# A graph network's gather kernel: products of layer 0 in two PSUM banks, their rows' copy in one, and later turns

## The chip, the cores and the metric

The kernel runs on one core of a Trainium2 chip. The metric is the device time of one execution in microseconds (us), lower is better; three runs of the kernel before gave a median of 2989.48 us (2987.55 to 3002.36). A core has five engines with a queue each: TensorE (PE in the profile, its weight loads PEld), VectorE (DVE), ScalarE (ACT), GpSimd (POOL) and SyncE (SP). They are tied together by semaphores: a counter that one engine raises and another waits for.

## The reference

Two graph layers over 6250 nodes with 512 features and 100000 edges sorted by target. Layer 0 sums each node's neighbours, and sends the sums through two dense products (512 to 1024 to 512) with a batch norm behind each; layer 1 has one product (512 to 512), a ReLU and a batch norm. Each ends in a residual and a row-wise layer norm.

```python
# layer 0
agg = segment_sum(x[src], dst, N);  h = (1 + eps) * x + agg
h = relu(batch_norm(h @ W1 + b1, g1, be1))
h = relu(batch_norm(h @ W2 + b2, g2, be2))
x = layernorm(x + (x + h))
# layer 1
agg = segment_sum(x[src], dst, N);  h = where(indeg > 0, agg, x)
h = relu(h @ W.T + b);  x = layernorm(x + batch_norm(h, gamma, beta))
```

## The kernel before

The program has five stages: `gather_phase` of layer 0, `hidden_phase` (the product with W2), `rows_phase` of layer 0, then `gather_phase` and `rows_phase` of layer 1.

**Gather.** Nodes come in 50 tiles of 125, worked off as 25 pairs. The edges come in 782 chunks of 128. For each chunk POOL issues one indirect DMA (L571) that fetches 128 rows of 512 numbers into one slot of a ring (34 slots in layer 0, 20 in layer 1). SP counts what has landed (L537). PE adds a chunk's rows to the tile's sums by a matmul with a selection matrix of zeros and ones (a tile looks at a window of 18 chunks), which DVE makes by comparisons (`selection`, L640 to L654). POOL may reuse a slot when PE's counter `used` says that its chunk is done (L586).

**Split rows.** A matmul in full fp32 takes four times the passes of one in the rounded format fp32r. So in layer 0 eight chunks of a window (two in layer 1) are split: ACT copies the rows rounded (`high_rows`, L929), and in layer 0 writes the same rounded rows once more into PSUM (L931, banks 5 and 7 in turn, `high_ps`); DVE subtracts that copy from the exact rows (`low_rows`, L670); PE multiplies both parts (L806, L811). The other ten chunks of a tile go as they are (L821, two records each in the profile). `AHEAD` says by how many rows ACT's copies may be ahead of DVE's subtractions: two, one for each bank. A tile's 18 steps stand in the order whole, whole, split, whole, split and so on, and end with a whole one.

**Turn and product.** When a pair's sums are complete, DVE adds the nodes' own rows (`read_sums`, L685). During the next pair, before step `TURN_AT` of its first tile, PE transposes them (`turn`, L839); ACT rounds the result (`high_part`, L916), DVE makes the low part (`low_part`, L693). The product with the layer's weights (`product`, L854) is cut into parts of 24 matmuls, four in layer 0 and two in layer 1, and `PRODUCT_AT` says behind which step of which tile each part stands. ACT reads a part out of PSUM (`read_product`, L943 and L946) and tells PE by `product_out` (L949); in layer 0 all parts use bank 4, so a part waits until the one before is read, while in layer 1 there are two banks. DVE takes the batch norm's statistics (L701). What an engine does in a pair is written out by hand, in L722 to L759 for DVE and L973 to L1011 for ACT; each engine works strictly in that order.

**Hidden and rows.** `hidden_phase` begins with the batch norm's constants (L1040: a square root on ACT), then rectifies the last pair's features, which are still on chip (`first`, L1126 for ACT and L1170 for DVE), and multiplies with W2 (L1214). `rows_phase` normalises blocks of features on ACT (`features`, L1323), PE turns them into rows (L1399), and DVE, ACT and POOL add the residual and do the layer norm.

## Time and profile before

| | |
|---|---|
| median of three runs | 2989.48 us (2987.55 to 3002.36) |
| the profiled execution's own time | 3012.35 us |
| its span, first to last instruction | 3010.6 us |
| granted TensorE clock, mean | 0.894 of full speed |
| PE busy, PEld busy | 81%, 54% |
| DVE, ACT, POOL busy | 46%, 32%, 51% |
| HBM | 181 GB/s over the span |

The profile is one execution. Busy shares are means over five stages with different limits, so a stage is read by itself: a window of the trace gives the busy time of each engine in it, the granted clock and the share of time in which the 16 DMA engines moved data. "Waited for" rows say how long an engine stood idle before an instruction and whose semaphore ended it; "issue" is idle time that no semaphore explains, and "remote" a semaphore whose raiser the profile did not find close by. The end of a matmul's record is modelled, its start is measured.

### The profile page before, as it was taken

What the parts mean: (1) busy time and instruction counts of PE and PEld (TensorE: products, weight loads), DVE (VectorE), ACT (ScalarE), POOL (GpSimd) and SP (SyncE); (2) the same over time, 40 slices, a digit from 0 to 9 for tenths busy, and PEclk for the clock granted to TensorE, in tenths of its full rate; (3) what the DMA queues carried; (4) which work ended last, traced back from release to release, by engine and by line L of the source; (5) the groups of instructions that cost most, each with busy time, mean ns of one, the idle gap of its engine ahead of it and who ended that gap; (6) DMA issues with size and microseconds to landing.
All of it is one profiled execution on the core that took longest, in us unless ns stands there. A gap on an engine that the chain in (4) does not pass through costs nothing. (4 is left out here: it accounts for less than half of the span.)

```text
span 3010.6 us, 42654 instructions
## 1 busy us (share of the span) xinstructions
PE 2427.2 (81%) x9711; PEld 1615.2 (54%) x9712; DVE 1370.1 (46%) x2159; ACT 955.1 (32%) x1674; POOL 1548.7 (51%) x1729
## 2 busy tenths in 40 slices
PE   3888778788887887799997497888779788877875
PEld 2555555556565655578886354444444444444445
DVE  4444444444443444453336554444344444444448
ACT  2444444444443443455555311010111011011026
POOL 6555656656555565500001465666566666666633
PEclk9989989999988898899998598989889898988986
DMA  7666656666666666632225765666666666666668
GB/s 242 183 194 185 206 170 203 191 204 188 202 184 195 181 205 184 184 94 95 95 95 151 248 189 171 184 183 177 177 180 181 190 183 183 188 180 180 175 175 270
DMA packets 180572, 545.12 MB, mean 181 GB/s; under 512 B 48787, under 2 KB 51178, under 8 KB 175794
## 3 DMA queue, kind: packets, MB, share of 16 engines
q0 software_dynamic: 125120, 410.09, 47.1%
q1 hardware_dynamic: 33880, 78.23, 8.8%
q10 hardware_dynamic: 21544, 56.48, 5.7%
q8 instruction: 11, 0.18, 0.0%
q14 instruction: 17, 0.14, 0.0%
HBM read 493.06 MB, written 51.62 MB: 181 GB/s over the span
## 5 line engine op out<-in xcount | busy, mean ns | idle before, releaser
L821 PE MATMUL psum<-ring,select 128*125 x2600 | 1270.1, 616 | 36.6 <-issue 36.4
L571 POOL DMA_INDIRECT ring<-x_in,staged x782 | 742.5, 950 | 522.9 <-issue 206.2
L571 POOL DMA_INDIRECT ring<-x_d,staged x782 | 751.3, 961 | 459.5 <-issue 219.7
L821 PEld LDWEIGHTS psum<-ring,select 128*125 128x125 f32 x2600 | 492.7, 196 | 440.7 <-issue 397.1
L854 PE MATMUL psum<-sumsT_hi,w_hi 128*128 128x250 f32 x1248 | 429.2, 344 | 244.8 <-ACTq L949 146.8
L670 DVE TENSOR_TENSOR rows_lo<-ring,psum 128x512 fp32r<-128x512 f32 x404 | 274.6, 686 | 425.4 <-ACT psum L931 352.5
L854 PEld LDWEIGHTS psum<-sumsT_hi,w_hi 128*128 128x128 f32 x1248 | 273.3, 219 | 318.7 <-ACTq L949 179.2
L929 ACT ACTIVATE rows_hi<-ring 128x512 fp32r x506 | 315.1, 628 | 315.0 <-issue 220.7
L854 PE MATMUL psum<-sumsT_lo,w_hi 128*128 128x250 f32 x1248 | 384.3, 308 | 7.0 <-issue 7.0
L854 PE MATMUL psum<-sumsT_hi,w_lo 128*128 128x250 f32 x1248 | 383.1, 307 | 7.6 <-issue 7.4
L806 PE MATMUL psum<-rows_hi,select_r 128*125 128x512 f32 x500 | 359.3, 719 | 13.1 <-issue 9.9
L854 PEld LDWEIGHTS psum<-sumsT_lo,w_hi 128*128 128x128 f32 x1248 | 275.4, 221 | 29.4 <-issue 29.3
L854 PEld LDWEIGHTS psum<-sumsT_hi,w_lo 128*128 128x128 f32 x1248 | 274.5, 220 | 6.1 <-issue 6.0
L943 ACT ACTIVATE of_layer<-psum,vecs 128x250 f32<-128x250 f32 x208 | 86.2, 466 | 494.2 <-remote 404.3
L931 ACT ACTIVATE psum<-ring 128x512 fp32r x404 | 236.6, 586 | 0.0
L916 ACT ACTIVATE sumsT_hi<-psum 128x500 fp32r<-128x500 f32 x104 | 55.5, 586 | 529.9 <-DMA ring<-x_in,staged 285.8
L1369 POOL TENSOR_TENSOR both_r<-six_r 125x5 f32<-125x5 f32 x18 | 3.6, 200 | 401.6 <-DVE six_r L1432 401.6
L681 DVE TENSOR_SCALAR lone<-psum 125x1 f32 (+1 forms) x51 | 8.1, 158 | 440.1 <-DMA x_d<-rows_r 203.3
L811 PE MATMUL psum<-rows_lo,select_r 128*125 128x512 f32 x500 | 202.0, 404 | 1.6 <-issue 1.6
L663 DVE TENSOR_REDUCE edge_count<-select 128x125 bf16<-128x2000 f32 x50 | 198.2, 3964 | 0.0
L946 ACT ACTIVATE h3T<-psum,vecs 128x250 f32 (+1 forms) x104 | 43.3, 468 | 478.1 <-DMA ring<-x_in,staged 365.0
L1214 PE MATMUL psum<-act_hi,w_hi 128*128 128x500 f32 (+1 forms) x416 | 160.3, 385 | 4.1 <-DVE act_lo L1172 4.1
(184 smaller groups left out, 2470.9 us busy)
## 6 DMA issues: line engine op xcount, KB each, us to landing
hidden_d<-of_layer ACTq DMA_DIRECT2D x25, 1000.0 KB
act_f<-hidden_d SPq DMA_DIRECT2D x24, 1000.0 KB
ring<-x_in,staged POOLq DMA_INDIRECT x782
ring<-x_d,staged POOLq DMA_INDIRECT x782
own<-x_in ACTq DMA_DIRECT2D x50, 224.0 KB
own<-x_d ACTq DMA_DIRECT2D x50, 224.0 KB
rows_r<-x_in SPq DMA_DIRECT2D x6, 1120.0 KB
x_d<-rows_r SPq DMA_DIRECT2D x6, 1120.0 KB
```

Source lines behind the costliest of these rows:

```text
L571: nc.gpsimd.indirect_dma_start(slot(s), None, table, bass.IndirectOffsetOnAxis(ap=staged[:, s:s + 1], axis=0)).then_inc(gathered[s], 16)
L663: nc.vector.tensor_reduce(edge_count[h][:, 1, :], select[h][:].rearrange("p k n -> p n k"), AX.X, ALU.add).then_inc(counted[h], 1)
L670: nc.vector.tensor_tensor(rows_lo[:, k, :], of_chunk(dve, first, SPLIT_AT[k]), high, ALU.subtract).then_inc(split_lo, 1)
L806: high = nc.tensor.matmul(agg(h), select_r[h][:, k, :], rows_hi[:, k, :], start=False, stop=False, skip_group_check=True)
L811: nc.tensor.matmul(agg(h), select_r[h][:, k, :], rows_lo[:, k, :], start=False, stop=False, skip_group_check=True).then_inc(split_used, 1)
L821: whole = nc.tensor.matmul(agg(h), select[h][:, WHOLE_AT.index(p), :], of_chunk(pe, first, place), start=False, stop=n + 1 == WINDOW, skip ...
L854: last = nc.tensor.matmul(out, w[:, k, o * P:(o + 1) * P], s[:, k, :], start=n == 0, stop=n == len(parts) - 1)
L916: nc.scalar.activation(sumsT_hi[:, b * z.KD // 2:(b + 1) * z.KD // 2, :], turn_ps[:, b, 0:z.W * z.KD // 2].rearrange("p (k n) -> p k n", n ...
L929: high = nc.scalar.activation(rows_hi[:, k, :], of_chunk(act, first, SPLIT_AT[k]), ACT.Copy)
L931: high = nc.scalar.activation(high_ps[k % 2].bitcast(F32R), of_chunk(act, first, SPLIT_AT[k]), ACT.Copy)
L943: nc.scalar.activation(hidden[:, o, :], from_, ACT.Identity, bias=m.b1[:, o:o + 1]).then_inc(out_done, 1)
L1214: last = nc.tensor.matmul(out, w[:, f * KK + k, o * P:(o + 1) * P], s[:, 0:pairs, k, :] if pairs == 2 else s[:, 0, k, :], start=f == 0 and ...
```

## The change

In layer 0 the parts of the product alternate between banks 4 and 7 (`prod_ps`), so that part b waits for the reading of part b-2; for that the rounded rows' copy in PSUM keeps bank 5 alone (`high_ps`), and ACT may be ahead of DVE by one row (`AHEAD` = 1). The turn stands before step 7 instead of 5 in layer 0 and before step 8 instead of 5 in layer 1. The parts of the product stand two steps later in layer 0; in layer 1 the first part goes from step 12 to the end of the first tile (18), the second from step 2 to step 6 of the second tile. ACT's readings and copies and DVE's subtractions, sums and statistics are put in another order to suit. A square root in setup has ACT's table loaded there. The first blocks of the hidden phase are handed from ACT to DVE to PE one by one, and in the rows phases the first four blocks of features are made by ACT (two), POOL and DVE.

The diff, cut to its core; in the order of its pieces: setup's square root, the steps, the banks, DVE's order in a pair, PE's wait for a bank, ACT's order in a pair, the hidden phase's first blocks on ACT, and the first blocks of the rows phases on POOL and DVE.

```diff
+        act.wait_ge(self.tables, 2)
+        nc.scalar.activation(self.root[:], m.bn_eps[:], ACT.Sqrt, bias=m.ln_eps[:, 0:1])
...
-    TURN_AT = 5
-    PRODUCT_AT = ({14: 0}, {2: 1, 8: 2, 14: 3}) if layer == 0 else ({12: 0}, {2: 1})
+    TURN_AT = 7 if layer == 0 else 8
+    PRODUCT_AT = ({16: 0}, {4: 1, 10: 2, 16: 3}) if layer == 0 else ({18: 0}, {6: 1})
...
-        high_ps = [m.bank(5), m.bank(7)]
-        AHEAD = 2 if layer == 0 else 0
-        PRODUCT_BANKS = 1 if layer == 0 else 2
-        def prod_ps(b, last):
-            return m.bank(4 if b % 2 == 0 or layer == 0 and not last else 0 if layer == 0 else 5)
+        high_ps = m.bank(5)
+        AHEAD = 1 if layer == 0 else 0
+        PRODUCT_BANKS = 2
+        def prod_ps(b):
+            return m.bank(4 if b % 2 == 0 else 7 if layer == 0 else 5)
...
-                            low_rows(v, 1, second, 0, 3)
+                            low_rows(v, 1, second, 0, 6)
                             read_sums(v, tiles(i, 0), 0)
-                            low_rows(v, 1, second, 3, 5)
...
-                            statistics(v, pair, 0, 2)
-                            low_rows(v, 1, second, 5, 7)
-                            statistics(v, pair, 2, 4)
-                            low_rows(v, 1, second, 7, SPLIT)
+                            low_rows(v, 1, second, 6, SPLIT)
+                            statistics(v, pair, 0, 4)
...
-                    pe.wait_ge(product_out, HALVES * job + b + (1 if layer == 1 or b == 0 or not final else 0))
+                    pe.wait_ge(product_out, HALVES * job + b + 1)
...
-                            high_rows(begin1, v, 1, second, 0, 3)
+                            high_rows(begin1, v, 1, second, 0, 4)
+                            load_own(v, tiles(i, 1), 1)
                             read_product(v, pair, 0)
-                            high_rows(begin1, v, 1, second, 3, 5)
-                            load_own(v, tiles(i, 1), 1)
+                            high_rows(begin1, v, 1, second, 4, 6)
                             read_product(v, pair, 1)
-                            high_rows(begin1, v, 1, second, 5, 7)
+                            high_rows(begin1, v, 1, second, 6, SPLIT)
...
+                            high_rows(following_begin, v + 1, 0, following, 0, 2)
                             read_product(v, pair, 2)
-                            high_rows(begin1, v, 1, second, 7, SPLIT)
-                            high_rows(following_begin, v + 1, 0, following, 0, EARLY)
+                            high_rows(following_begin, v + 1, 0, following, 2, EARLY)
                             read_product(v, pair, 3)
...
+                    for k in range(KK + 1):
+                        if k < KK:
+                            nc.scalar.activation(m.hidden[:, f * KK + k, :], m.hidden[:, f * KK + k, :], ACT.Relu,
...
+                        if k:
...
+                            nc.scalar.activation(act_hi[f][:, 0, k - 1, :], m.hidden[:, f * KK + k - 1, :], ACT.Copy
+                                                 ).then_inc(hi_done[f] if k == KK else first_hi, 1)
...
+        def first_features(engine, wait, k, line, done):
+            out = normed[0][:, k, :]
+            made = engine.tensor_scalar(out, featT[:, k, 0:SW], scale[:, k:k + 1], bias[:, k:k + 1], ALU.mult, ALU.add)
+            if layer == 0:
+                made.then_inc(line, 1)
+                wait.wait_ge(line, 1)
+                made = engine.tensor_scalar(out, out, 0.0, None, ALU.max)
+            made.then_inc(done, 1)
```

What this moves in the queues shows at three places. On PE, in the first tile of a pair in layer 0, ahead of the turn (L790 and L839 follow these rows; `rows_hi` and `rows_lo` are the split rows, `select_0` a tile's selection):

```order
 L821 MATMUL psum<-ring,select_0 125x512
 L805 ISA
+L806 MATMUL psum<-rows_hi,select_r_0 125x512
+L811 MATMUL psum<-rows_lo,select_r_0 125x512
+L820 REGISTER_ALU
+L821 ISA
+L821 MATMUL psum<-ring,select_0 125x512
+L805 REGISTER_ALU
 L806 MATMUL psum<-rows_hi,select_r_0 125x512
 L811 MATMUL psum<-rows_lo,select_r_0 125x512
```

One split and one whole step more stand in front of the turn; the same step pairs have gone from behind it, from in front of the product's parts.

On ACT, in the second tile of a pair in layer 0: L929 and L931 are one split row's two copies, L943 the reading of one part of the product (`of_layer` is where it goes), L910 the load of the tile's own rows. Before:

```order
L929 ACTIVATE rows_hi<-ring 128x512
L931 ACTIVATE psum<-ring 128x512
...
L943 ACTIVATE of_layer<-psum,vecs 128x250 x2
...
L929 ACTIVATE rows_hi<-ring 128x512
L931 ACTIVATE psum<-ring 128x512
...
L929 ACTIVATE rows_hi<-ring 128x512
L931 ACTIVATE psum<-ring 128x512
...
L910 DMA own_0<-x_in 112x512
L910 ISA
L910 DMA own_0<-x_in 13x512
...
L943 ACTIVATE of_layer<-psum,vecs 128x250 x2
```

and after:

```order
L929 ACTIVATE rows_hi<-ring 128x512
L931 ACTIVATE psum<-ring 128x512
L910 ISA
L910 DMA own_0<-x_in 112x512
L910 ISA
L910 DMA own_0<-x_in 13x512
...
L943 ACTIVATE of_layer<-psum,vecs 128x250 x2
...
L929 ACTIVATE rows_hi<-ring 128x512
L931 ACTIVATE psum<-ring 128x512
...
L929 ACTIVATE rows_hi<-ring 128x512
L931 ACTIVATE psum<-ring 128x512
...
L943 ACTIVATE of_layer<-psum,vecs 128x250 x2
```

The first reading now stands behind the tile's fourth split row instead of its third, the load of own rows stands in front of it, and the second reading is behind the sixth row instead of the fifth.

On ACT at the start of the program and of the hidden phase (L1040 is the square root of the batch norm's variance):

```order
+L215 ACT_TABLE_LOAD
+L215 ACTIVATE setup_root<-bn_eps,ln_eps 128x1
...
-L1040 ACT_TABLE_LOAD
 L1040 ACTIVATE bn_tmp<-bn_tmp,bn_eps 128x8
```

There are two table loads before and one after, which has moved from in front of the first copy of setup to in front of the added root.

## Rows read from the trace of the kernel before

**Rows 1.** Windows of the trace: the two gather stages, from first turn to last.

```profile
core 0: us, PE busy (x) PEld busy (x) DVE busy (x) ACT busy (x) POOL busy (x), PEclk, DMA share, GB/s
53.20:1270.10 1216.90, 982.38 (x4273) 679.57 (x4274) 531.24 (x912) 520.14 (x1010) 708.68 (x748) 0.91 0.65 192
1762.60:2913.20 1150.60, 948.66 (x3207) 529.72 (x3206) 508.87 (x671) 121.70 (x240) 709.69 (x739) 0.90 0.63 180
```

**Rows 2.** Timeline of PE (start us, us, engine line op): turns of layer 0's last pairs.

```profile
1270.11 1.91 PE L839 MATMUL psum<-ident,sums 125*128 125x125 f32 x8
...
1306.54 1.05 PE L839 MATMUL psum<-ident,sums 125*128 125x125 f32 x8 [1.02 <-DVE sums L685]
```

**Rows 3.** Waits (us in total, times, longest) of PE: layer 0's gather, then layer 1's.

```profile
PE psum L854 <- ACTq L949: 146.8, 33, 10.5
PE psum L790 <- DVE sums L685: 60.5, 15, 5.4
...
PE psum L854 <- DVE sumsT_lo L693: 77.4, 12, 10.5
PE psum L790 <- DVE sums L685: 41.8, 5, 11.2
```

**Rows 4.** Waits of POOL in layer 0's gather.

```profile
POOL ring L571 <- PE psum L821: 162.7, 66, 10.8
POOL ring L571 <- remote: 149.0, 51, 4.3
```

**Rows 5.** Timeline around layer 0's third product of a pair, with gathers running.

```profile
637.21 0.68 PE L854 MATMUL psum<-sumsT_hi,w_hi 128*128 128x250 f32 x1
640.27 0.28 PE L854 MATMUL psum<-sumsT_hi,w_lo 128*128 128x250 f32 x1
...
644.72 0.95 POOL L571 DMA_INDIRECT ring<-x_in,staged  x1 [0.30 <-issue]
...
647.45 0.83 ACT L943 ACTIVATE of_layer<-psum,vecs 128x250 f32<-128x250 f32 x2 [9.00 <-remote]
...
648.38 0.38 PE L854 MATMUL psum<-sumsT_hi,w_hi 128*128 128x250 f32 x1 [3.87 <-ACTq L949]
648.41 0.95 POOL L571 DMA_INDIRECT ring<-x_in,staged  x1 [2.74 <-remote]
```

**Rows 6.** Timeline around a first product after the last gather.

```profile
1281.93 0.28 PE L854 MATMUL psum<-sumsT_hi,w_lo 128*128 128x250 f32 x1
...
1282.25 0.47 ACT L943 ACTIVATE of_layer<-psum,vecs 128x250 f32<-128x250 f32 x1 [0.89 <-PE psum L854]
```

**Rows 7.** Timeline of ACT and DVE: split rows, back to back and one by one.

```profile
615.05 0.63 ACT L929 ACTIVATE rows_hi<-ring 128x512 fp32r x1 [2.11 <-issue]
616.11 0.61 ACT L929 ACTIVATE rows_hi<-ring 128x512 fp32r x1
...
620.99 1.28 DVE L670 TENSOR_TENSOR rows_lo<-ring,psum 128x512 fp32r<-128x512 f32 x2
...
621.97 0.63 ACT L929 ACTIVATE rows_hi<-ring 128x512 fp32r x1 [2.35 <-DVE rows_lo L670]
622.51 0.59 ACT L931 ACTIVATE psum<-ring 128x512 fp32r x1
...
623.29 0.69 DVE L670 TENSOR_TENSOR rows_lo<-ring,psum 128x512 fp32r<-128x512 f32 x1 [1.02 <-ACT psum L931]
```

**Rows 8.** Timeline: ACT's first row after the loop's end; DVE's selection begins.

```profile
608.97 0.63 ACT L929 ACTIVATE rows_hi<-ring 128x512 fp32r x1 [1.86 <-issue]
...
618.01 0.23 DVE L640 TENSOR_SCALAR local<-dst_t,tile_bases 128x17 f32 x1
```

**Rows 9.** Timeline of the hidden phase's start.

```profile
1326.86 1.28 ACT L1040 ACT_TABLE_LOAD   x1 [4.06 <-PEq L88]
...
1329.34 2.06 ACT L1128 ACTIVATE of_layer<-of_layer,bias,scale 128x250 f32<-128x250 f32 x4 [0.87 <-DVE bias L1037]
...
1333.85 0.55 PE L1214 MATMUL psum<-act_hi,w_hi 128*128 128x250 f32 x1 [4.10 <-DVE act_lo L1172]
```

**Rows 10.** Timeline of PE: the rows phase's first transposes, layer 0.

```profile
1618.86 3.40 PE L1399 MATMUL psum<-ident,normed_r 128*125 128x128 f32 x14 [8.25 <-ACT normed_r L1325]
```

78 lines of the change are left out of this document (52 added, 26 removed).

## The prediction, made before the changed kernel was run

> **What bounds the kernel now.** I read the busy shares by slice first: two gather stages, one for each layer, take almost 80% of the span (1216.9 and 1150.6 us, PE's clock at 0.91 and 0.90 of full, DMA share 0.65 and 0.63) [rows 1]. Layer 0's runs from its first turn to its 25th, so 24 pairs at 1216.9 / 24 = 50.7 us; layer 1's 1150.6 / 24 = 47.9 us. PE is recorded busy for 982.4 of 1216.9 us. The waits say what it misses: 146.8 us for ACT's reading of the one product bank (ACTq L949) and 60.5 us for the sums that the turn needs; in layer 1, 77.4 us for the low part of the turned sums and 41.8 us for sums [rows 3].
>
> The timeline shows why. A product's 24 matmuls start at 637.21 and the last is recorded at 640.27; ACT, which has waited 9.00 us for its completion, starts to read at 647.45, and PE, which has gone on with gathered rows meanwhile, stands 3.87 us before the next product [rows 5]. POOL's last gather of that stretch starts at 644.72, the next at 648.41 after 2.74 us of waiting. So a product's completion is told some 7 us after its last record, shortly after the gather stream has run dry, and everything starts again then. After the last gather, a product whose last record is at 1281.93 is read at 1282.25, 0.3 us later [rows 6], and that whole pair takes 1306.54 - 1270.11 = 36.4 us [rows 2]. Hence 50.7 - 36.4 = 14.3 us of a pair are these late completions and what follows from them. POOL alone needs 1.25 us a gather (0.95 and 0.30 [rows 5]): 748 gathers in 24 pairs [rows 1] are 31.2 a pair, 39.0 us, and its waits are (162.7 + 149.0) / 24 = 13.0 us more [rows 4]; together about the pair's 50.7.
>
> I take the lateness as a fact of this kernel without knowing its cause. One rule speaks against reading it as idle time: the Trainium skill (Trace Analysis, "Tensor Engine Instruction") says that a matmul's end in the profile is computed, and that the semaphore moves only when PSUM has acknowledged all bytes. By that rule the array could still be working until 647.4, and a second bank would give nothing; that is rival C. Rows 2 and 6 speak against it, since the same work ends promptly and 14.3 us sooner without gathers.
>
> **Layer 0, what goes.** Two product banks let product b start once b-2 is read. Between products lie six steps of gathered rows plus a product, so the wait of 146.8 / 24 = 6.1 us a pair is mostly gone. The wait before the turn stays: the third product and the turn both move by two steps, their distance is the same, and the chain behind it (read, statistics, sums) is unchanged: 60.5 / 24 = 2.5 us a pair.
>
> **Layer 0, what comes.** The rounded rows' copy has one bank, so ACT's pair of copies for row k+1 waits until DVE has subtracted row k. Before, pairs follow each other every 616.11 - 615.05 = 1.06 us. One by one they cost [rows 7]: the pair from 621.97 to 622.51 + 0.59 = 623.10, 1.13 us; 0.19 us until DVE starts at 623.29; 0.69 us of DVE; and 0.3 us until ACT starts again (DVE's pair of rows from 620.99 has its first end near 621.68, ACT starts at 621.97). Sum 2.31 us, times 16 rows: 37.0 us. What lies between the rows, less what runs beside the other engine's part:
> - ACT's way round the loop, 1.86 us [rows 8] instead of 0.3, and DVE's sums: 1.8 us.
> - Turn, its high and low part: 1.0 to 2.7 us (the upper end is the 2.11 us that ACT stands before 615.05 [rows 7]).
> - DVE's two selections, each from 618.01 to 620.99, 3.0 us [rows 7, 8], of which the next copy hides 1.1 to 1.5; the second follows the sums and a register load: 1.5 + 3.1 us.
> - Four reads of products (0.83 us each [rows 5], each half hidden by a subtraction) and statistics: 1.3 us.
>
> Together 45.7 to 47.4, say 46.5 us a pair. This chain of ACT and DVE, hardly visible before (25 of 50 us), is now longer than POOL's 39.0 and PE's own work, below 36.4. It is the new bound.
>
> On top come completions that it can't cover. Reads stand 4 to 10 us behind their products in the new order, so the first three mostly fit (7 us late against 9 to 12 us of distance), while the fourth is read at once after the last row: some 2 to 3 us stay. I take 46.5 + 2.2 = 48.7 us. Bounds: 45.7 (all covered) and 46.5 + 7 = 53.5 (one full lateness of 7.2 us a pair on the chain). Against 50.7 that is -2.0 us (-5.0 to +2.8), over 24 pairs -48 us (-120 to +67). The last pair, without gathers, goes from 36.4 to about 46: +10 us. Layer 0: -38 us (-110 to +77).
>
> **Layer 1.** Turn from step 5 to 8, first product from 12 to the tile's end, second from 2 to 6; it had two banks already. PE comes 3 steps, some 2.6 us, later to the turn and 5.2 us later to the product, so the 77.4 us of waits for the low part (12 times, longest 10.5) and the 41.8 us for sums (5 times) [rows 3] shrink by at most 12 x 5.2 + 5 x 2.6 = 75 us. But work is only moved: POOL's 39 us and its pauses stay, and selection for the second tile, queued on DVE behind the low part, starts 2.6 us later with 3 us. It is covered by the product now in front of that tile. I take a third: -24 us (-60 to +10).
>
> **The short phases.** The square-root table is loaded in setup beside other waits; in front of the hidden phase it stood in the open for 1.28 us [rows 9], and the next instruction starts at its end: -1.3. The Trainium skill (ScalarE: Activation LUTs, "What ACT_TABLE_LOAD costs") puts a switch at 2.66 us with its drain; by that figure 1.4 us more would go, but the row shows no drain. Hidden phase: PE starts at 1333.85, 4.5 us after ACT's first block at 1329.34 [rows 9]; with blocks handed on singly it can start after two blocks, a copy and a subtraction, about 2 us, but then waits for each of the four: -1.5 (0 to -2.5). Eight small copies instead of two cost ACT up to 1 us, hidden by PE's first unit. Rows phases: PE waits 8.25 us for four ACT blocks [rows 10], of which two now go to DVE and POOL: -2 each (-1 to -2.5). Sum -7 us.
>
> **Sum.** -38 - 24 - 7 = -69 us on the profiled execution, whose own time is 3012.4 us (span 3010.6): 2943. The runs' median is 2989.5, a factor 0.992 below it, so 2921 us.
>
> **Rivals.**
> A, the forecast: the copy chain replaces the bank wait and is a little shorter. 0.45; 2921 us.
> B, slower: the single copy bank decides. If a product's completion on the ACT-DVE chain costs its whole lateness once a pair, the period is 53.5 us: +67 + 10 in layer 0. For it speaks that ACT reads in program order, so each late product stops all later copies and with them PE; against it, the new distances. It decides from a period of 50.7 us, 4.2 us of uncovered waiting on 46.5. With the other terms (-24 - 7) 3012 + 46 = 3058, median terms 3035 us. 0.25.
> C, nothing moves: the array is busy until the completion, as in the rule above, or the stream of gathers keeps its 39.0 + 13.0 us whatever PE does, because each product still ends in a pause. Layer 0 at 50.7, layer 1 unchanged, -7: 2983 us. Four products a pair and four pauses speak for it. 0.13.
> D, a large gain: PE runs on to the next product while the last is late, so that one pause flushes two, the chain covers all, period 46.0, and layer 1 gains 60: -113 + 10 - 60 - 7 = -170: 2821 us. Against it: each late product also freezes the counters that POOL and ACT wait for. 0.17.
>
> **Numbers.** 0.5% (15 us) is what a measurement of this kernel can tell from no change. Faster: 0.42 of A and all of D, 0.59; same: 0.03 of A and 0.11 of C, 0.14; slower: B and the rest of C, 0.27. Range: A's bounds alone are 2850 to 3000; with most of B and half of D, 2840 to 3038.
>
> **What would show it.** Right: the rows of PE's wait for ACTq L949 in layer 0 nearly gone; ACT's copy pairs at about 2.3 us, each begun by DVE's L673; PE waiting instead for rows_lo and for sums; turns 48 to 49 us apart; the pair after the last gather longer, near 46 us. Wrong: copies still close to 1.1 us apart (DVE never the releaser), or turns below 46 or above 51 us apart; in layer 1 the wait for the low part still at 77 us; a table load still in front of the hidden phase.

## The result and the profile after

The changed kernel took 2959.3 us (median of four, 2952.64 to 2964.52) against 2989.64 us for the kernel before on the same chip: a ratio of 0.9896, 95% interval 0.9869 to 0.9922. So it is faster, by 30 us, where 69 were forecast (2921 us). The experiments add a second finding that the forecast did not see coming: two chips were met in a second condition, in which the kernel before needs only 2498 us, and there the same change makes it 5.8% slower.

The profiled execution of after took 2964.52 us (span 2962.8). Its two gather stages and the last pair, as busy times in windows from turn to turn, against [rows 1, 2]:

```profile
core 0: us, PE busy (x) PEld busy (x) DVE busy (x) ACT busy (x) POOL busy (x), PEclk, DMA share, GB/s
60.58:1234.52 1173.94, 985.48 (x4274) 662.71 (x4274) 533.18 (x912) 529.11 (x1010) 704.40 (x746) 0.92 0.67 198
1234.52:1277.15 42.63, 32.79 (x165) 22.50 (x163) 22.09 (x38) 21.74 (x42) 0.00 (x0) 0.96 0.10 30
1735.58:2865.16 1129.58, 949.21 (x3201) 530.01 (x3199) 504.72 (x670) 119.24 (x240) 707.66 (x736) 0.90 0.63 182
```

Layer 0 has 1173.94 / 24 = 48.9 us a pair (before 50.7, forecast 48.7), its last stretch, without gathers, 42.6 (36.4; about 46), layer 1 1129.58 / 24 = 47.1 (47.9). The first turn comes at 60.58 instead of 53.19 us. Two things about these marks. The first turn already stands in the first pair, ahead of its step 5 (now 7), and the last one behind the last pair's end, so the last stretch holds 31 of a pair's 36 steps before and 29 after, not a whole pair. And a turn that is moved to a later step moves the mark with it. Of the 26 turns of a stage, layer 0's windows run from the first to the 25th, layer 1's from the second to the last; those of [rows 1] do so too. What PE waits for has changed its name as forecast; its waits in layer 0 and then in layer 1 (us in total, times, longest), against [rows 3]:

```profile
PE psum L854 <- issue: 60.6, 45, 2.6
...
PE psum L806 <- DVE rows_lo L673: 31.2, 11, 8.6
PE psum L790 <- DVE sums L688: 30.3, 10, 5.1
...
PE psum L854 <- issue: 106.4, 81, 2.5
...
PE psum L790 <- DVE sums L688: 18.8, 5, 6.0
PE psum L854 <- DVE sumsT_lo L696: 13.5, 4, 7.2
```

ACTq L949 (146.8 us) is gone from layer 0. In layer 1 the waits for the low part fell from 77.4 to 13.5 us and those for sums from 41.8 to 18.8, but PE now stands inside its products, with no semaphore to name: L854 "issue" is 106.4 us where before's waits in the same stage have

```profile
PE psum L854 <- issue: 14.7, 15, 1.9
```

The idle time has moved with PE's place in the program; little of it has gone.

ACT's timeline shows the chain of one copy bank: in the first tile of a pair L929 begins 2.32 and 2.41 us apart ([rows 7]: 1.06 us when free), in the second one a row names DVE's subtraction as what it waited for, and further on a reading still waits 4.13 us for its completion.

```profile
602.98 0.63 ACT L929 ACTIVATE rows_hi<-ring 128x512 fp32r x1
...
605.30 0.63 ACT L929 ACTIVATE rows_hi<-ring 128x512 fp32r x1 [1.19 <-issue]
...
607.71 0.63 ACT L929 ACTIVATE rows_hi<-ring 128x512 fp32r x1 [1.29 <-issue]
...
631.45 0.63 ACT L929 ACTIVATE rows_hi<-ring 128x512 fp32r x1 [1.19 <-DVE rows_lo L673]
...
646.15 0.83 ACT L943 ACTIVATE of_layer<-psum,vecs 128x250 f32<-128x250 f32 x2 [4.13 <-remote]
```

The starts of the short phases, ACT and PE in the hidden phase and PE in the rows phase of layer 0, against [rows 9, 10]:

```profile
1299.10 0.30 ACT L1040 ACTIVATE bn_tmp<-bn_tmp,bn_eps 128x8 f32<-128x8 f32 x1 [4.08 <-DVEq L1029]
1300.28 1.08 ACT L1131 ACTIVATE of_layer<-of_layer,bias,scale 128x250 f32<-128x250 f32 x2 [0.87 <-DVE bias L1037]
1301.27 0.40 ACT L1141 ACTIVATE act_hi<-of_layer 128x250 fp32r<-128x250 f32 x1
...
1302.26 0.36 PE L1234 MATMUL psum<-act_hi,w_hi 128*128 128x250 f32 x1 [0.28 <-DVE act_lo L1184]
...
1583.21 8.93 PE L1430 MATMUL psum<-ident,normed_r 128*125 128x128 f32 x40 [5.87 <-ACT normed_r L1371]
1598.90 4.70 PE L1430 MATMUL psum<-ident,normed_r 128*125 128x128 f32 x20 [6.75 <-ACT normed_r L1358]
```

No table load stands there any more, and PE starts 1302.26 - 1300.28 = 2.0 us after ACT's first block instead of 4.5. In the rows phase PE waits 5.87 instead of 8.25 us, but then 6.75 us for the next block. Before, the second run of transposes began 12.9 us after the first (1618.86 to 1631.76), now 15.7: the 2.4 us are given back within 16 us.

### The profile page after: what moved, and what is told of

It reads as the page before. It is cut to its first block and busy times, and to the rows that moved or that the text cites. A ratio compares the mean times of both kernels' runs of the same rounds, so it can differ in the third digit from the quotient of the medians.

```text
span 2962.8 us, 42669 instructions
## 1 busy us (share of the span) xinstructions
PE 2431.3 (82%) x9711; PEld 1596.7 (54%) x9712; DVE 1374.3 (46%) x2168; ACT 956.8 (32%) x1676; POOL 1551.7 (52%) x1732
## 5 line engine op out<-in xcount | busy, mean ns | idle before, releaser
L821 PE MATMUL psum<-ring,select 128*125 x2600 | 1299.2, 623 | 68.2 <-issue 58.6
L821 PEld LDWEIGHTS psum<-ring,select 128*125 128x125 f32 x2600 | 495.2, 198 | 467.0 <-issue 421.7
L929 ACT ACTIVATE rows_hi<-ring 128x512 fp32r x506 | 314.8, 630 | 605.2 <-issue 316.7
L854 PE MATMUL psum<-sumsT_hi,w_hi 128*128 128x250 f32 x1248 | 432.9, 347 | 74.4 <-issue 60.7
L854 PE MATMUL psum<-sumsT_hi,w_lo 128*128 128x250 f32 x1248 | 372.4, 298 | 58.7 <-issue 58.6
L854 PE MATMUL psum<-sumsT_lo,w_hi 128*128 128x250 f32 x1248 | 373.8, 299 | 51.1 <-issue 47.8
L854 PEld LDWEIGHTS psum<-sumsT_hi,w_hi 128*128 128x128 f32 x1248 | 260.1, 208 | 123.0 <-issue 105.3
L854 PEld LDWEIGHTS psum<-sumsT_lo,w_hi 128*128 128x128 f32 x1248 | 261.7, 210 | 102.3 <-issue 102.1
L854 PEld LDWEIGHTS psum<-sumsT_hi,w_lo 128*128 128x128 f32 x1248 | 262.8, 211 | 56.7 <-issue 56.7
L931 ACT ACTIVATE psum<-ring 128x512 fp32r x404 | 236.0, 584 | 0.0
L916 ACT ACTIVATE sumsT_hi<-psum 128x500 fp32r<-128x500 f32 x104 | 55.4, 584 | 534.4 <-DMA ring<-x_in,staged 336.0
L806 PEld LDWEIGHTS psum<-rows_hi,select_r 128*125 128x125 f32 x500 | 98.3, 197 | 189.3 <-issue 140.6
L673 DVE TENSOR_TENSOR rows_lo<-ring,rows_hi 128x512 fp32r<-128x512 f32 x102 | 66.5, 688 | 243.4 <-ACT rows_hi L929 141.8
```

The costliest lines, as they stand in the source:

```text
L673: nc.vector.tensor_tensor(rows_lo[:, k, :], of_chunk(dve, first, SPLIT_AT[k]), high, ALU.subtract).then_inc(split_lo, 1)
L806: high = nc.tensor.matmul(agg(h), select_r[h][:, k, :], rows_hi[:, k, :], start=False, stop=False, skip_group_check=True)
L821: whole = nc.tensor.matmul(agg(h), select[h][:, WHOLE_AT.index(p), :], of_chunk(pe, first, place), start=False, stop=n + 1 == WINDOW, skip ...
L854: last = nc.tensor.matmul(out, w[:, k, o * P:(o + 1) * P], s[:, k, :], start=n == 0, stop=n == len(parts) - 1)
L916: nc.scalar.activation(sumsT_hi[:, b * z.KD // 2:(b + 1) * z.KD // 2, :], turn_ps[:, b, 0:z.W * z.KD // 2].rearrange("p (k n) -> p k n", n ...
L929: high = nc.scalar.activation(rows_hi[:, k, :], of_chunk(act, first, SPLIT_AT[k]), ACT.Copy)
```

## The experiments

Every kernel was compared with the kernel before on its own chip. The table has all runs, with stage times from the turns in each profile. Layer 0's period is the mean of the 24 stretches that follow its first turn; "last pair" is the last stretch; "short" runs from the last turn of layer 0 to the first of layer 1; layer 1's period is the mean of its last 24 stretches, the very last of which is again a part of a pair. The kernels n_before and n_after leave out most gathers, and h_after, d2 and d3 leave out half of each row that they gather.

| kernel | before there | ratio (95%) | first turn | layer 0 period | last pair | short | layer 1 period |
|---|---|---|---|---|---|---|---|
| before | 2989.6 | 1 | 53.2 | 50.70 | 36.4 | 419.8 | 47.94 |
| after | 2989.6 | 0.9896 (0.9869-0.9922) | 60.6 | 48.91 | 42.6 | 420.9 | 47.07 |
| e1 short phases | 2982.8 | 0.9972 (0.9951-0.9993) | 52.8 | 50.51 | 36.0 | 415.3 | 47.34 |
| e2 layer 1 | 2982.8 | 0.9964 (0.9944-0.9983) | 52.7 | 50.11 | 35.7 | 420.9 | 47.01 |
| e3 layer 0 | 2982.8 | 0.9931 (0.9906-0.9956) | 58.2 | 48.51 | 41.9 | 422.8 | 47.41 |
| e4 banks, old steps | 2982.8 | 1.0054 (1.0031-1.0077) | 56.2 | 50.13 | 42.8 | 421.9 | 47.58 |
| e5 steps, old banks | 3016.2 | 1.0000 (0.9983-1.0017) | 55.4 | 51.05 | 33.2 | 417.9 | 47.15 |
| e6 no PSUM copy | 3016.2 | 0.9805 (0.9779-0.9831) | 53.0 | 48.86 | 35.6 | 420.2 | 47.25 |
| n_before, no gathers | 3016.2 | 0.7958 (0.7929-0.7987) | 55.6 | 36.82 | 34.3 | 422.2 | 36.19 |
| n_after, no gathers | 3016.2 | 0.8527 (0.8495-0.8560) | 60.0 | 43.57 | 42.8 | 417.6 | 36.07 |
| g1 layer 0 as before | 2987.3 | 0.9960 (0.9944-0.9977) | 55.3 | 50.26 | 36.0 | 414.6 | 47.00 |
| g2 half the copies | 2987.3 | 0.9826 (0.9804-0.9847) | 55.1 | 48.45 | 33.2 | 416.6 | 46.72 |
| c1 after again | 2497.8 | 1.0581 (1.0566-1.0595) | 58.7 | 43.76 | 42.8 | 415.5 | 39.12 |
| c2 = e6 | 2497.8 | 1.0140 (1.0125-1.0156) | 53.4 | 39.65 | 36.4 | 414.5 | 39.12 |
| c3 e6, other order | 2497.8 | 1.0140 (1.0125-1.0156) | 53.8 | 39.58 | 36.0 | 413.8 | 39.16 |
| h_after, half rows | 2497.8 | 1.0489 (1.0470-1.0508) | 55.9 | 43.59 | 42.8 | 415.0 | 38.48 |
| d1 before again | 2498.8 | 0.9999 (0.9990-1.0008) | 52.9 | 38.12 | 36.5 | 415.3 | 39.24 |
| d2 before, half rows | 2498.8 | 0.9948 (0.9929-0.9966) | 53.6 | 38.16 | 37.1 | 417.0 | 38.56 |
| d3 after, half rows | 2498.8 | 1.0503 (1.0484-1.0522) | 58.1 | 43.56 | 42.8 | 417.9 | 38.55 |
| d4 e4, no PSUM copy | 2498.8 | 1.0153 (1.0139-1.0167) | 51.0 | 39.68 | 36.1 | 415.9 | 39.23 |

### The three parts alone: e1, e2, e3

e1 takes all of the diff but the gather stages; e2 is before with two lines changed, e3 before with layer 0's part of the gather function:

```diff
-    TURN_AT = 5
-    PRODUCT_AT = ({14: 0}, {2: 1, 8: 2, 14: 3}) if layer == 0 else ({12: 0}, {2: 1})
+    TURN_AT = 5 if layer == 0 else 8
+    PRODUCT_AT = ({14: 0}, {2: 1, 8: 2, 14: 3}) if layer == 0 else ({18: 0}, {6: 1})
```

> Only the short phases changed: root table in setup, first blocks of the hidden phase handed on singly, first features by ACT, POOL and DVE; both gather phases as before. Forecast's account: -7 us (1.3 for the table load, 1.5 in the hidden phase, 2 in each rows phase), 2982 us. Rival that fits the changed kernel's profile (its stretch between last turn of layer 0 and first turn of layer 1 is 420.9 us against 419.8): what starts earlier is given back before the phase ends, 0 us (-2 to +2), 2989 us. A third: the added root in setup delays the first turn by the 7.4 us seen there, +6 us. In the profile: PE's first product with W2 starts 2 us sooner after ACT's first block if the handing-on works (before 4.5 us).

> Only layer 1's steps changed (turn before step 8 instead of 5, product parts behind step 18 and step 6 of the second tile instead of 12 and 2). Forecast's account: -24 us, 2965 us, the 77 us of PE's waits for the low part of the turned sums mostly gone. The changed kernel's profile gave -21 us from first to last turn (1150.5 to 1129.6): theory 1, that is the change's own, 2969 us. Rival: before's profiled execution was 23 us above its median and part of this difference was that excess, so that the change alone gives -5 us or less, 2985 us, with the turns 47 us apart in both.

> Only layer 0's gather changed (two product banks, one bank for the rounded rows' copy, turn and parts two steps later, the new order on ACT and DVE); layer 1 and the short phases as before. Forecast's account: -38 us, 2952 us. Theory 1 (the changed kernel's profile, period 50.7 to 48.9, first turn 7.4 us later, last pair 6.2 us longer): -30 us, 2960 us. Theory 2 (layer 0's typical period before was below the profiled 50.7, near 50.0): -10 to -15 us, 2977 us; then the sum of the single changes is the -30 us of the medians. A first turn near 60 us instead of 53 would say that the start belongs to this part.

Measured: -8.4, -10.7 and -20.6 us (ratios times 2983), together -40, in keeping with the whole change's -31 (-39 to -23). e1 (-14.6 to -2.1) agrees with the forecast's -7. The table's "short" averages 421.4 us in four kernels with the old starts (before, e2, e3, e4) and 417.6 in six with the new ones (after, e1, e5, e6, g1, g2), -3.8; but its end, the first turn of layer 1, stands three steps later in five of the six. Up to the first gathered row of layer 1 (the first record of L821 there) the averages are 414.7 and 409.3 us, -5.4. From layer 1's last turn to the end of the program both average 97.3 us, so the new start of layer 1's rows phase, for which 2 us were forecast, shows nothing. The idea that the added root delays the first turn is refuted (52.8 us in e1). e2 (-16.7 to -5.1) is half of the forecast. Its windows of both stages show why a single trace misled: layer 0, which e2 leaves alone, is 14 us shorter here than in the trace of before [rows 1].

```profile
52.70:1255.34 1202.64, 980.50 (x4273) 674.18 (x4274) 531.13 (x912) 519.19 (x1010) 707.52 (x749) 0.91 0.65 194
1750.43:2878.63 1128.20, 953.01 (x3201) 522.25 (x3199) 505.87 (x671) 119.36 (x240) 706.18 (x735) 0.90 0.63 182
```

Layer 1's 24 pairs take 1150.5 us in before's trace, but 1136.2, 1137.7 and 1141.8 in e1, e3 and e4, which don't change it; the four average 1141.6. With the new steps they take 1128.7 on average (after, e2, e5, e6, g1, g2). Of these -13 us, two things take a part back: the window now begins three steps later, and the stage's first stretch, outside it, is up to 4 us longer (36.3 us with the old steps, 36.3 to 40.6 with the new ones). From the first gathered row of the stage to its last turn it takes 1183.9 us with the old steps (four kernels) and 1175.7 with the new ones (six): -8 us. The largest waits of PE in layer 1, first of e1 and then of e2:

```profile
PE psum L858 <- DVE sumsT_lo L697: 80.7, 12, 11.7
PE psum L794 <- DVE sums L689: 41.5, 7, 8.2
PE psum L794 <- issue: 28.4, 6, 9.0
PE psum L858 <- issue: 18.6, 17, 6.5
```

```profile
PE psum L854 <- issue: 85.5, 67, 3.1
...
PE psum L854 <- DVE sumsT_lo L693: 26.7, 8, 11.5
PE psum L790 <- DVE sums L685: 12.2, 3, 6.1
```

In e1 (old steps; its L858 and L794 are before's L854 and L790) PE stands 80.7 + 41.5 + 28.4 = 150.6 us ahead of products and sums and 18.6 inside products; in e2 40.4 ahead (with 1.5 us of "issue" at L790) and 85.5 inside. Of 110 us that went, 67 came back inside the products and 18 more in front of whole rows (L821 "issue", 10.0 and 27.6 us). PE's busy time is 11.6 us longer in e2 besides (953.0 against 941.4 us, granted clock 0.90 against 0.91).

### Layer 0's two halves: e4 and e5

e4 is before with the banks alone; e5 is the changed kernel with the old banks:

```diff
-        high_ps = [m.bank(5), m.bank(7)]
-        AHEAD = 2 if layer == 0 else 0
-        PRODUCT_BANKS = 1 if layer == 0 else 2
+        high_ps = m.bank(5)
+        AHEAD = 1 if layer == 0 else 0
+        PRODUCT_BANKS = 2
```

> Before, with the banks alone changed in layer 0: products alternate between two banks and the rounded rows' copy has one; all steps and both engines' orders as before. If the second product bank is what pays (forecast: PE's 146.8 us of waits for the reading of the one bank go) and the copy chain costs what it does in the changed kernel, it is faster, -25 us, 2965 us. Rival: the banks alone cost, because the readings stand only 2 to 6 us behind their products in the old order, so that the lateness of completions falls on a copy chain without slack: period 53.5 us, +67 us, 3056 us. Copy pairs 2.3 us apart either way; 1.1 us apart would show that the chain isn't there.

> The changed kernel with the old banks in layer 0: one product bank, two banks for the rounded rows' copy; all steps and orders new. Theory 1 (the second product bank pays in layer 0): the waits for the reading of the one bank come back, layer 0 at 50.7 us a pair or above, +30 to +45 us on the changed kernel, 2990 to 3005 us. Rival (the new positions pay, the banks only swap one wait for another of the same size): within 5 us of the changed kernel, 2955 to 2965 us, with copies 1.1 us apart again.

Neither half gains: the banks alone cost 0.5%, and the steps alone (with the other two parts' 0.6% in it) leave layer 0 0.6% slower. In e4 PE's waits for sums are 85.6 us in 18 places and 35.0 with "issue" ([rows 3]: 60.5), while its gaps before products are 67.0 us instead of 146.8 for the bank; its trace has the 24 pairs no longer than those of before (50.1 against 50.4 us on average), and the first turn and the last stretch 3 and 7 us longer. In e5 the bank wait is back (e4, then e5):

```profile
PE psum L789 <- DVE sums L684: 85.6, 18, 5.6
PE psum L853 <- issue: 67.0, 58, 2.2
PE psum L789 <- issue: 35.0, 7, 5.1
```

```profile
PE psum L855 <- ACTq L950: 132.8, 35, 9.6
PE psum L807 <- DVE rows_lo L674: 38.1, 7, 6.3
PE psum L791 <- DVE sums L689: 35.2, 11, 5.3
```

The two belong together, which the forecast had not priced. That the later turn is what makes room for the chain of the second bank fits e4's waits for sums, but isn't shown: the steps and both engines' orders were changed together.

### What sets the pair's time: no gathers, no copy

n_before and n_after raise the ring's counters without fetching (the gathers after the ring's first round are left out, so their sums are of the wrong rows). e6 takes the copy into PSUM out of the changed kernel:

```diff
-        AHEAD = 1 if layer == 0 else 0
+        AHEAD = 0
...
-                        high = high_ps if layer == 0 else rows_hi[:, k, :].bitcast(F32)
+                        high = rows_hi[:, k, :].bitcast(F32)
...
-                        if layer == 0:
-                            high = nc.scalar.activation(high_ps.bitcast(F32R), of_chunk(act, first, SPLIT_AT[k]),
-                                                        ACT.Copy)
```

> Leaves out all gathers but the first round of the ring in both layers (sums are of the wrong rows; every other instruction stays, the counters are raised by SP as before). The pair's time without gathers, kernel before. Forecast's account: 36.4 us a pair in layer 0 (the last pair's time), so that 14.3 us of a pair are late completions and what follows: 24 x 14.3 = -343 us in layer 0 alone. Completions told 0.3 us after the last matmul's record. Rival: the last pair was short for want of other work (its own rows, selections) or for a full clock, and the period without gathers stays at 42 us or more.

> The same with the changed kernel: leaves out all gathers but the first round of the ring. Forecast's account: the chain of ACT and DVE alone sets the period, 46.5 us (45.7 to 47.4); measured for the last pair 42.6 us, which is theory 1. So 8 to 10 us a pair slower than the kernel before without gathers, though faster with them. Rival: a period like that of before without gathers (36 to 38 us), which would say that the chain isn't a bound and the 48.9 us with gathers are set by the gather stream.

> The changed kernel, but DVE subtracts the rounded rows from ACT's copy in on-chip memory, as layer 1 does, and the second copy into PSUM isn't made: two product banks and no lockstep. ACT's work falls by 0.58 us and the handover is free of the one bank for 400 rows. If the chain of ACT and DVE (2.31 us a row, 16 rows a pair) bounds layer 0, its period falls from 48.9 to 46 us, -70 us, 2890 us. Rival: DVE with both operands outside PSUM takes longer or holds up POOL's gathers (0.95 us each), and PE is stopped by late completions all the same: 0 us or up to +60 us. In the profile: DVE's subtraction 0.69 us before, POOL's gather 0.95 us before, copies less than 2.3 us apart.

Without gathers the kernel before needs 36.8 us a pair, PE busy throughout; the changed one 43.6, and its window shows PE at 936 of 1046 us:

```profile
55.60:939.37 883.77, 883.77 (x4274) 613.21 (x4274) 527.08 (x914) 516.94 (x1012) 0.00 (x0) 1.00 0.12 43
```

```profile
60.00:1105.53 1045.53, 936.29 (x4273) 629.78 (x4274) 529.96 (x912) 526.61 (x1010) 0.00 (x0) 0.96 0.10 35
```

So the chain of ACT and DVE exists and costs 43.6 us, 3 less than the forecast's 46.5. But the chain alone doesn't set 48.9: e6 has none, and its layer 0 still takes 48.86 us. One thing clouds this: POOL's gathers in layer 0 take 1011 ns in e6 and 946 in the changed kernel, 65 ns times 31.2 or 2.0 us of POOL's time a pair, so that the chain may hold up to some 2 us of the 48.9. e6 gains elsewhere, at the first turn (53.0 instead of 60.6) and in the last pair (35.6 instead of 42.6), 14.5 of its some 27 us ahead of the changed kernel (0.9805 against 0.9896, on different chips). The difference at the first turn is the chain too, since e6 leaves out the copy and its waits and nothing else: the copies of the first tile's rows stand ahead of that turn one by one. Its size is 7.5 us here and 5.3 in a second pair of traces (58.7 in c1, 53.4 in c2).

### The two conditions: c1 to c3, the half rows, d1, d4

> The changed kernel unchanged, on the chip of the next kernels, to compare with them and to see how far one execution's stages differ from another's. Theory 1 (the single changes add: ratios 0.9972, 0.9964 and 0.9931 against before, product 0.987): 0.985 to 0.992 of before. Layer 0 between 48.4 and 49.0 us a pair and layer 1 between 47.0 and 47.3; rival: the gain of the first measurement was that chip's or that run's, and here it is under 0.5%.

> The kernel without the copy into PSUM (DVE subtracts ACT's copy in on-chip memory) again, beside the changed kernel on one chip. Theory 1 (the one copy bank costs the first pair 7.6 us and the last 7 us, and inside the loop the chain's 43.6 us is covered, so that the period stays what it is): -15 us against the changed kernel, 0.995 of it. Rival (the chain bounds the loop): -15 us and 2 us a pair more, -60 us.

> The kernel without the copy into PSUM, and ACT makes the second tile's last four rounded rows in one go ahead of the second reading (before: two, the reading, two). Theory: what is left of layer 0's waits is late completions that ACT waits for in program order with copies queued behind them (PE waited 48.6 us for rows in 9 places, longest 8.9): those go, -1 to -2 us a pair, -20 to -50 us against the kernel without this reorder. Rival: the gather stream sets the pace, and PE's waits only change their place: within 10 us.

> The changed kernel, but after the ring's first round each gather fetches 256 of a row's 512 numbers (leaves out half of the data; POOL issues as many gathers of 128 rows, PE and all else do the same work). Without any gathers layer 0 takes 43.6 us a pair and layer 1 36.1; with whole ones 48.9 and 47.1. Theory 1 (the bytes that the DMA engines move set the lateness of completions and PE's pauses): layer 1 near 41 us, POOL's own 39.0 us the bound, layer 0 near 45; about 2720 us. Rival (the number of gathers and POOL's stream set them, whatever the bytes): 48 and 47 us as before, 2950 us.

All four expected times fell, for a reason that lies outside the kernel (c1 is the changed kernel, unchanged): the chip on which before had taken 3016 us in the series of e5, e6 and the kernels without gathers took 2498 us for it in the next series, and 2643 for the changed kernel. Before has no trace from that series, so I took a second one of it, on another chip, where it was 2498 us again. Below, "late completions" is the first condition (near 3000 us) and "prompt completions" the second; a completion is the semaphore that tells that a matmul's result can be read.

> The kernel before, unchanged, for a second trace of it. On one chip it has taken 3016 us and, a few minutes later, 2498 us, and the changed kernel 2643 us then, 5.8% more: so the time depends on a condition of the chip that the kernel doesn't set. Theory: where completions come promptly each gather stage runs at its longest engine chain (before: POOL's 39.0 us a pair in both layers; changed: ACT and DVE's 43.6 us in layer 0), and where they come late every kernel is near 48 to 51. So this trace shows either 39 us a pair in both layers, about 2500 us, with no wait of PE for ACTq's reading of the bank; or 50.1 to 50.7 and 47.3 to 47.9, about 2990 us. Rival: values between, which would say that the condition is one of degree.

> The kernel before, but after the ring's first round each gather fetches 256 of a row's 512 numbers (leaves out half of the data). Where completions come late: theory 1 (the bytes moved set the lateness) 43 to 46 us a pair in layer 0 and near 42 in layer 1, about 2750 us; rival (the number of gathers or of descriptors does) 50 and 47, 2980 us. Where they come promptly: POOL's 39.0 us, no more than 1% below the kernel before, since 16 DMA engines at a share of 0.75 aren't its bound.

> The changed kernel with half rows, for the condition in which the kernel before takes 2990 us. There: theory 1 (bytes) near the chain's 43.6 us in layer 0, 2700 us; rival 48.5 us, 2950 us. In the other condition it took 2620 us.

> Before, with two product banks in layer 0 and DVE subtracting ACT's copy in on-chip memory (no copy into PSUM, no lockstep); all steps and orders of before, layer 1 and the short phases unchanged. Late completions: theory (the bank wait of 146.8 us goes and no chain takes its place) 0.985 of before, and 1 us a pair below the kernel with two banks and one copy bank (50.1 us); rival (PE's waits only change their name) 1.00. Prompt completions: POOL's gather takes 1.00 instead of 0.95 us beside DVE's reads, so 0.5 to 1.4% slower than before.

d1's windows of layer 0 and 1, then its waits of PE in layer 0, then its timeline at the end of a product there, with a gather of POOL in its midst:

```profile
52.88:967.72 914.84, 892.62 (x4273) 608.99 (x4274) 525.35 (x912) 521.60 (x1007) 690.57 (x731) 1.00 0.82 250
1455.77:2397.48 941.71, 895.70 (x3206) 476.51 (x3205) 511.00 (x671) 125.68 (x240) 711.89 (x736) 1.00 0.76 218
```

```profile
PE psum L790 <- DVE sums L685: 9.3, 8, 2.5
...
PE psum L854 <- ACTq L949: 5.3, 12, 0.5
```

```profile
400.62 0.28 PE L854 MATMUL psum<-sumsT_hi,w_lo 128*128 128x250 f32 x1
400.70 0.95 POOL L571 DMA_INDIRECT ring<-x_in,staged  x1 [0.30 <-issue]
400.93 0.83 ACT L943 ACTIVATE of_layer<-psum,vecs 128x250 f32<-128x250 f32 x2 [2.11 <-PE psum L854]
```

The reading starts 0.31 us after the start of the product's last record, in the midst of gathers; in [rows 5] it was 7 us. Over layer 0, ACT's readings that had to wait (more than 0.3 us) began a median of 5.1 us after that start in the trace of before (87 readings) and 0.31 us in d1's (47) and in n_before's (54). The kernel is the same, and so are the instructions of the other engines (POOL's gather 0.95 us in both). PE's are not: the same 4273 records are busy for 892.6 us in d1 and 982.4 in [rows 1], at granted clocks of 1.00 and 0.91. So 90 of the 302 us between the two windows, 3.7 us a pair, are PE's own work taking longer at a lower clock. In the stretch of [rows 5] PE stands idle until 648.38, and from 649.84 to 653.25 its granted clock is 0.50 (1.2 instead of 2.4 GHz), after 1.00 before. PE's wait for the bank is 5.3 us in all instead of 146.8.

That the product's own work doesn't fill the late 7 us can be read in the trace of before too, whose PE goes on with gathered rows: twelve of their records, the last two in this line, start between the product's last record (640.27) and its reading (647.45).

```profile
643.49 1.02 PE L821 MATMUL psum<-ring,select 128*125 x2
```

With prompt completions each pair lasts as long as its longest chain of work: POOL's in before (38.1 and 39.2 us), ACT and DVE's in layer 0 of the changed kernel (43.76, its time without gathers, 43.57). c1's waits of PE in layer 0 name that chain and nothing else:

```profile
PE psum L790 <- DVE sums L688: 82.2, 25, 3.4
PE psum L806 <- DVE rows_lo L673: 31.1, 28, 1.5
```

24 x (43.76 - 38.12) = 135 us, 5.8 at the first turn and 6.3 in the last pair, less 2 between the layers and 0.6 in layer 1: 145, as measured (2643.4 - 2497.8 = 145.6). Layer 1's new steps give next to nothing here: from its first gathered row to its last turn the stage takes 983.6 us in d1 and 983.0 in c1.

With prompt completions the bytes matter little: half rows take 13 us off before (0.9948), all of it in layer 1, and none of it in layer 0. Whether late completions go with the bytes stays open, since every half-row run met prompt ones. The other order on ACT (c3) gave nothing there and was not tried with late ones; d4, at 1.5% above before, is just past the 0.5 to 1.4% expected.

c2 and d4 show what leaving out the PSUM copy costs: with both of DVE's operands in SBUF, the on-chip memory outside PSUM, each of POOL's gathers in layer 0 takes longer, while those of layer 1, the same in both, don't. First d1's groups, then c2's:

```profile
L571 POOL DMA_INDIRECT ring<-x_d,staged x782 | 756.6, 967 | 250.1 <-issue 218.8 <-PE psum L821 13.1 <-POOLq L88 9.7
L571 POOL DMA_INDIRECT ring<-x_in,staged x782 | 741.5, 948 | 244.6 <-issue 224.5 <-PE psum L821 14.4 <-DVEq L374 3.2
```

```profile
L574 POOL DMA_INDIRECT ring<-x_in,staged x782 | 781.4, 999 | 243.9 <-issue 223.3 <-PE psum L819 11.9 <-DVEq L378 4.4
L574 POOL DMA_INDIRECT ring<-x_d,staged x782 | 755.1, 966 | 249.5 <-issue 217.9 <-PE psum L819 12.7 <-POOLq L88 9.7
```

c1, which differs from c2 by the copy and its waits alone, has 947 ns in layer 0, and d4 997. 51 ns x 748 gathers = 38 us; layer 0 of c2 is 24 x (39.65 - 38.12) = 37 us longer, with POOL the bound. The Trainium skill (SBUF — State Buffer, "Who interferes with whom") says that a DVE instruction with two SBUF inputs contends with a GpSimd instruction that reads SBUF, and that one with at most one such input, outside VectorE's two-port modes, does not; POOL's gathers read their row numbers (`staged`) from SBUF, and these traces agree.

### The last two: g1 and g2

g1 keeps layer 0 as before beside the rest of the change. g2 copies every second row into PSUM:

```diff
-        AHEAD = 1 if layer == 0 else 0
+        AHEAD = 2 if layer == 0 else 0
...
-                        high = high_ps if layer == 0 else rows_hi[:, k, :].bitcast(F32)
+                        high = high_ps if layer == 0 and k % 2 == 0 else rows_hi[:, k, :].bitcast(F32)
...
-                        if layer == 0:
+                        if layer == 0 and k % 2 == 0:
```

> Layer 0's gather as before (one product bank, two copy banks, old steps); layer 1's new steps and the short phases' new starts kept. Where completions come promptly: layer 0 stays at 38.1 us a pair instead of the changed kernel's 43.8, so 0.997 of before (-3 us in layer 1, -3 in the short phases, 2491 us), against 1.058 for the changed kernel. Where they come late: 0.9972 x 0.9964 = 0.9936 of before. Rival: layer 1's new steps cost something with prompt completions (PE reaches its product at the tile's end and the pair's sums later), 1.002 or more.

> The changed kernel, but only every second rounded row is copied into PSUM; DVE subtracts the others from ACT's copy in on-chip memory. Two product banks, and ACT may run two rows ahead, so no lockstep. Prompt completions: theory (the lockstep alone makes the changed kernel 5.8% slower, and DVE's reads in on-chip memory make POOL's gather 0.05 us longer in proportion to their number) 38.9 us a pair, 1.003 to 1.008 of before, between before and the version without any copy (1.014). Rival: the alternation still holds ACT to DVE's pace, 41 us or more, 1.03. Late completions: 0.980 to 0.985 of before, as the version without any copy.

Both met late completions. g1: 0.996 against the 0.9936 of e1 times e2, each known to 0.002; its short stretch (414.6) and its layer 1 (47.00) are those of the new code. What it does with prompt completions, where its forecast was 0.997, was not measured. g2: 0.9826, as expected, and so ahead of the changed kernel by 0.7% (its interval ends below where that of after begins, on two chips); first turn 5.4 us earlier, last pair 9.4 us shorter, the 24 pairs of layer 0 11 us shorter. POOL's gather is 983 ns, between 946 (after) and 1011 (e6), both with late completions:

```profile
L574 POOL DMA_INDIRECT ring<-x_in,staged x782 | 768.7, 983 | 445.4 <-issue 208.8 <-remote 127.2 <-PE psum L821 101.0
```

Its time with prompt completions was not measured either.

## Why the prediction was right or wrong

**In short.** The kernel became faster, as forecast, but by 30 us instead of 69. Two terms failed: layer 1's gain, taken as -24 us where the runs show -8 to -11, and the stretch up to layer 0's first turn, put at nothing where it is +5.9. The account of layer 0's new bound failed too, with its number met by luck.

**What bounds the kernel.** The late completions and the size of what they cost a pair were right: 36.8 us without gathers, and 38.1 with gathers and prompt completions, against 50.4 on average with late ones. The 14.3 us came out by luck in part: the 36.4 us of [rows 2] were read as a whole pair and hold 31 of its 36 steps (n_before's last stretch is 34.3 us where its pairs take 36.8). And "what follows from them" holds a term that the forecast didn't name, the lower granted clock, 3.7 of the 12.3 us. That they come with the gathers was half of it: they need the gathers (n_before, in a series with late completions, has none) and a condition of the chip besides (d1 has the gathers and not the lateness). Rival C's reading, that the array still works until the semaphore, is hard to hold: in d1 the same product is told 0.31 us after its last record starts, and in the trace of before twelve later records start ahead of the semaphore. What holds it back was not found.

**Layer 0's mechanism.** The wait for the bank went, the copies stand 2.3 us apart, PE waits for rows and sums, and the period is 48.9 us where 48.7 was forecast. But the step "it is the new bound" failed with late completions: the chain is 43.6 us, not 46.5, and without it (e6, with POOL's gathers 2.0 us a pair longer) the period is the same. It holds with prompt ones, where the pair takes 43.8 us. That 48.7 was met is luck: two errors cancelled, 3 us too much chain and 3 us too little lateness (5.1 instead of 2.2). What the runs show in its place is a toll of lateness on each kernel's own time: 50.4 - 38.1 = 12.3 us in before (mean of before, e1, e2, g1), 48.7 - 43.8 = 5.0 in the changed one (after, e3), 48.9 - 39.7 = 9.2 in e6. PE's lower clock is a part of it, 3.7 us in before and 1.9 in the changed kernel (985.5 us busy in after, 939.8 in c1). The second bank and the later steps took 7.3 us off the toll, the lockstep of ACT and DVE at the one bank put 5.6 on the work: -1.7 a pair, -40 us for the 24.

**Its ends.** The stretch up to the first turn was missing from the sum, put at nothing without a reason: +5.9 us (53.5 on average before, 59.4 after). Most of it is the chain; some 2 us are the turn's own move by two steps (e5, with the new steps and the old banks, has 55.4), which the last stretch has less. That stretch was sized +10 and is +6.2, or some +8 without the move; the chain's 3 us are the rest. Layer 0 in all is -28 us by the traces and -21 (-28 to -13) by e3's ratio, forecast -38.

**Layer 1, the term that failed most.** Forecast -24, measured -8 by the traces and -11 (-17 to -5) by e2's ratio, a third to a half of it. The step that failed is "I take a third": a third of 75 us of waits was taken for a gain. The waits ahead of sums and products did shrink, by 110 us in e2, but 67 of them reappeared as gaps inside the products and 18 ahead of whole rows. Here a wait that a late completion causes was not removed by reaching it later.

**Short phases.** -7 forecast, -8.4 (-14.6 to -2.1) by e1's ratio, -5.4 by the traces. The table load is gone from its place (1.28 us [rows 9]), and PE's start in the hidden phase came 2.5 us nearer, where 1.5 was taken. The rows phase of layer 0 gives its 2.4 us back within 16 us, and that of layer 1 shows no gain.

**The scale.** The sum of the traces' terms is -28 - 8 - 5 = -41, that of the three ratios -40, and the medians differ by 30 (-39 to -23); that last gap stays open. The forecast subtracted its terms from an execution 23 us above its median, and 16 of those 23 lay in the very stages from which the terms were read (layer 0 7 us above the mean of four kernels with the same code, layer 1 9). The factor 0.992 spread them over the whole, terms and rest alike.

**The rivals.** None of the four is what happened. B's mechanism, a chain that decides and makes the kernel slower, is what happens with prompt completions, at 43.8 against 38.1 us a pair, and the forecast had no case for a chip on which most of the 14.3 us simply isn't there.

## What to carry to other kernels

Here waits that ended with a completion that nothing in the kernel explained were a property of the run, not a budget. So measure the kernel again, on another chip or later, before spending work on hiding them, because what hides them (here a bank taken from the copies) costs its full price when they are absent. Ahead of trading one resource for another, work out each engine's chain without the wait; if the new chain is longer than the other engines' (43.6 against POOL's 38 to 39), the trade can only pay while the wait lasts. Check what a mark between stages holds: here the window from turn to turn showed -13 us in layer 1, and the whole stage had gained 8. And take the size of a term from two executions of the same code, not from one, when the term is a per cent of the span.

## What the runs showed of the hardware

- The same kernel on the same chip took 3016 and, minutes later, 2498 us (medians of 17 and 9 runs, each within 1%). In the traces of the longer case the reader of a product started some 7 us after the start of its last record (median 5.1 over layer 0), and gaps of 1 to 3 us stood inside runs of matmuls; in the shorter one (d1) it started 0.31 us after it. Instructions of POOL, ACT and DVE are as long in both; PE's records take 982 against 893 us in layer 0, at a granted clock of 0.91 against 1.00. What switches the condition was not found.
- DVE's subtraction with both operands in SBUF lengthens POOL's gathers by 51 ns each with prompt completions (948 to 999) and by 65 with late ones (946 to 1011); with every second copy in PSUM it was 37 ns (983).
- Halving a gather's bytes left POOL's 0.95 us an issue and the pair's time in layer 0 as they were (38.16 against 38.12 us), and took 1.7% off layer 1's, all with prompt completions.
- An ACT to DVE handover through a single PSUM bank costs 2.3 us a row of 128x512, against 1.06 us back to back with two.
